# A graph attention kernel whose gather queue gets a memset and a drain after every gather

## The reference

```
edge layer 0 (4 heads of 32): kj = k[src] + e;  alpha = sum(q[dst] * kj) * scale
    softmax of alpha over the edges of each dst
    out[dst] = sum over edges of (v[src] + e) * alpha        then gate, project, layernorm -> x1
edge layer 1 (1 head of 256): scores = sum(q[dst] * k[src]) * scale + edge_weight * we + be
    softmax over the edges of each dst
    out[dst] = sum over edges of v[src] * attn               then layernorm, FFN, layernorm, layernorm
```

## Time and profile before

| | us |
|---|---|
| median of 3 executions | 5529.07 |
| lowest and highest | 5522.97, 5533.86 |
| span of the profiled execution | 6986.8 |
| of it before the first gather | 162.7 |
| first gather of phase 0 to its last | 3119.0 |
| from there to the first gather of phase 1 | 313.3 |
| first gather of phase 1 to its last | 2987.1 |
| from there to the end | 404.7 |
| busy: PE, DVE, POOL, ACT | 4413.6, 4304.2, 3716.2, 1729.7 |

### The profile page before, as it was taken

One profiled execution on the slowest core, in us unless ns is written; L12 is line 12 of the kernel. 1 busy time (PEld: TensorE's weight loads), 2 busy tenths in 40 slices (PEclk: granted clock), 3 DMA queues, 4 the chain that ended last, 5 costly groups with the idle time before them and its releaser, 6 DMA issues.

```text
span 6986.8 us, 104716 instructions
## 1 busy us (share of the span) xinstructions
PE 4413.6 (63%) x26899; PEld 3604.4 (52%) x26899; DVE 4304.2 (62%) x14756; ACT 1729.7 (25%) x4276; POOL 3716.2 (53%) x3934
## 2 busy tenths in 40 slices
PE   5565656565555556556656666666666666666698
PEld 3455555555555555555434555444454445555577
DVE  5456655566555556556855666666665666666688
ACT  0344544444444444445210000000000000000032
POOL 1555555555555555554135555556555555555455
PEclk9677776677777677777877778888887878878899
DMA  5565655555555555554345666556666666665422
GB/s 156 150 161 156 162 158 153 152 153 159 156 152 152 153 153 158 156 160 129 110 128 149 159 157 158 157 156 159 154 163 152 154 153 160 159 159 158 123 78 71
DMA packets 777208, 1039.58 MB, mean 149 GB/s; under 512 B 206912, under 2 KB 528273, under 8 KB 776609
## 3 DMA queue, kind: packets, MB, share of 16 engines
q1 hardware_dynamic: 466736, 499.53, 28.0%
q0 software_dynamic: 169040, 436.01, 23.3%
q10 hardware_dynamic: 140832, 97.33, 4.4%
HBM read 929.76 MB, written 128.40 MB: 151 GB/s over the span
## 4 chain that ended last, share of the span: by engine, by line
DVE 31%; PE 21%; another core or an unknown queue 19%; issue 15%; DVEq 6%; DMA 3%; POOL 3%; ACT 2%; ACTq 1%; POOLq 0%; SPq 0%
PE ps L1275 19%; DVE oh L1055 4%; DVE prod L925 4%; DVE rows L902 4%; POOL rows L580 3%; DVE acc L1075 2%; DVE score L914 2%; DMA acc_d<-acc 2%; DVEq L1133 2%; DVE msg L1050 2%; DVE oht L893 2%; DVE prod L909 1%; DMA rows<-x_d,idx 1%; DVEq L339 1%
## 5 line engine op out<-in xcount | busy, mean ns | idle before, releaser
L580 POOL DMA_INDIRECT rows<-kv_d,idx x1760 | 1709.4, 971 | 1552.0 <-DVE score L914 818.6
L580 POOL DMA_INDIRECT rows<-x_d,idx x1760 | 1767.7, 1004 | 1222.5 <-DVE score L925 581.2
L1275 PE MATMUL ps<-qw,oht 128*128 128x128 bf16 (+2 forms) x12320 | 1372.0, 267 | 230.4 <-issue 199.7
L1275 PEld LDWEIGHTS ps<-qw,oht 128*128 128x128 bf16 x12320 | 1125.8, 113 | 507.7 <-issue 294.2
L1275 PE MATMUL ps<-rows,oh 128*128 128x257 f32 x3520 | 1093.1, 469 | 421.8 <-DVE oh L1055 275.0
L1275 PEld LDWEIGHTS ps<-rows,oh 128*128 128x128 f32 x3520 | 789.9, 234 | 587.9 <-DVE oh L1055 302.3
L925 DVE CUSTOM_DVE_ANT_0 prod<-rows,ps 128x256 f32<-128x256 f32 x1760 | 637.1, 418 | 653.3 <-remote 229.6
L1275 PE MATMUL ps<-msg,oh 128*128 128x132 f32 x3520 | 679.0, 348 | 507.4 <-issue 296.1
L1275 PEld LDWEIGHTS ps<-msg,oh 128*128 128x128 f32 x3520 | 582.8, 246 | 575.2 <-issue 360.0
L699 ACT ACTIVATE pen_r<-ps 128x128 f32<-128x128 f32 (+1 forms) x110 | 29.9, 272 | 3051.3 <-PE ps L1355 2249.1
L1275 PE MATMUL ps<-w_c,ea 128*128 128x128 f32 x3520 | 691.0, 350 | 146.7 <-issue 103.3
(11 more groups left out here) (201 smaller groups left out, 4423.7 us busy)
## 6 DMA issues: line engine op xcount, KB each, us to landing
dst_row<-in_dst_row SPq DMA_DIRECT2D x880, 256.0 KB
qw<-q_d SPq DMA_DIRECT2D x440, 192.8 KB
acc_d<-acc ACTq DMA_DIRECT2D x440, 128.5 KB
ea<-in_eaT SPq DMA_DIRECT2D x440, 128.0 KB
qw<-q_d SPq DMA_DIRECT2D x440, 96.0 KB
acc_d<-acc ACTq DMA_DIRECT2D x440, 66.0 KB
rows<-kv_d,idx POOLq DMA_INDIRECT x1760
rows<-x_d,idx POOLq DMA_INDIRECT x1760
```

Of the source, the lines that this page charges most:

```text
L580: pool.indirect_dma_start(out=L.rows[par][:, st, j, 0:D], out_offset=None, in_=L.table, in_offset=bass.IndirectOffsetOnAxis(ap=idx[par][:, ...
L1275: return pe.matmul(out_, lhsT=lhsT, rhs=rhs, start=first, stop=last)
```

## The change

POOL gets a new buffer `spacer` of 128x384 f32 in SBUF, which nothing reads. After each gather, so 3520 times, it writes zeros to it and drains.

```diff
+SPACER = 384
...
+        spacer = sb("spacer", [P, SPACER])
...
                                 in_offset=bass.IndirectOffsetOnAxis(ap=idx[par][:, st, j:j + 1], axis=0),
                                 bounds_check=None if L is L0 else N - 1, oob_is_err=L is L0)\
                                 .then_inc(s["gathered"][b], 16)
+                            pool.memset(spacer[:, :], 0.0)
+                            pool.drain()
                 chunks(pool, emit)
```

## The result

The changed kernel takes 14469.66 us (14465.66 to 14484.62), the kernel before 5526.67 us beside it. The ratio is 2.619, 95% interval 2.616 to 2.623.

A forecast was written before the change was run, and what follows sets the result against it. The prediction took POOL as nearly full in both edge phases. Gathers of 4.7 and 4.8 us plus 0.3 us a pair gave 8404 and 8580 us, with 881 outside 17,865, rounded to 17,850; range 14,800 to 20,000.

The forecast's parts named there:

- the first rival: Drain in the loop waits only for POOL itself, not for the gather's packets: 8,500 us, chance 0.08.
- The preparation of 0.70 us: Ahead of each gather behind a drain, the next gather's preparation shows in full: 0.70 us in phase 0.
- some 1.3 us more: At each gather's drain: it ends 1.3 us after the gather's last packet, read from the drains ending both phases.
- The lower bound of 3.13 us: Gather start to drain end, calm case, from the last gather of phase 1; gave the total of 14,800 us.
- the drain ends with the landing: Rival for each gather's drain: it ends at the landing, 3.31 and 3.41 us a gather; 13,000 us, chance 0.05.
- 0.3 us a pair for the waits in the open: Ahead of each pair of four gathers, POOL's four waits and their arithmetic no longer hidden: 0.3 us, an estimate.
- Preparation in phase 1 of 0.80: Ahead of each phase 1 gather, preparation taken as 0.80 us because a bound for its indices is also set.
- Start to last packet 2.7 (2.5 + 0.2): Each gather's data is moved 2.5 us after its start, plus 0.2 us for meeting SP's loads.
- Outside the phases 881: Time ahead of, between and behind the two stretches of gathers, taken as unchanged: 881 us.
- The 0.2 us that I added for loads: Added to each gather's start to drain end, since some meet SP's loads on the same DMA engines: 0.2 us.
- The gathers that meet loads: Rival that every gather meets loads and takes 3.54 us to land, 5.6 and 5.7 in all: 20,900 us, chance 0.04.
- Not slower: Rival that the 0.30 us gap between gathers and POOL's room absorb memset and drain: 5,530 us, chance 0.01.

The follow-up runs named there:

- the second profile: The kernel before, unchanged, profiled once more: span 5549.3 us beside a time of 5550.99 us.

## Why the prediction was wrong

**What held.** POOL becomes the only bound, and the time is its distance between gathers times 3520 and the 861 us outside. The memset lies under the wait for the gather's data (the drain alone gives the same time, and so nearly do four memsets). The drain waits for the gather's transfer, not for POOL alone: the first rival's 8,500 us is far off. The preparation of 0.70 us is open behind each drain, to the hundredth. That POOL was nearly full before, which I argued from the plain time against the waits of the profile, is shown by the second profile and by the memsets of 256 and 384 columns.

**The step that failed.** "It waits until the gather's data has moved, and some 1.3 us more." The 1.34 and 1.33 us were measured right, but at drains with 1760 gathers ahead of them. I took them for a fixed part of every drain. The tail is 0.072 us behind the landing with one gather, grows by 0.04 us with each further one up to the 32 that were tried, and is 1.0 to 1.2 us at the end of a stage of the kernel before; between last packet and landing lie another 0.34 to 0.38 us. In the changed kernel the drain ends 0.44 us behind the last packet (mean), so 0.86 us too many stood in each of 3520 gathers: 3,030 us. The lower bound of 3.13 us from start to drain end came from such a drain too, with a tail of 1.21 us in it. Nor was it a calm gather, as I had it: it was one that moved no rows. From the gather's start to 6583.90 us POOL's DMA queue shows only 96 packets with 0.00 MB, all under 512 bytes:

```profile
q0 software_dynamic: 96, 0.00, 3.4%
```

By its semaphore the gather landed 1.95 us after its start. A short landing and a long tail happened to add up to 3.13. In the changed kernel the start to the drain's end takes 2.84 and 2.89 us in the median and 3.11 and 3.09 in the mean. That is why 14,800 was too high for a bound.

The first drain of line 239 was the hint. It has two transfers ahead of it, and ends 2.89 us after the start of the second (2.84 by the rounded rows), which took 2.76 us to land: a tail of 0.13 us, between those of one gather and of four. From it I made a rival, "the drain ends with the landing", at 13,000 us with a chance of 0.05. Its mechanism is the right one; its price took 2.61 us for the landing, from one of the two rows that I had (2.61 and 3.54), where the mean is 3.0.

**Smaller terms.** 0.3 us a pair for the waits in the open: 0.15 (130 us). Preparation in phase 1 of 0.80: 0.76 (70 us). Start to last packet 2.7 (2.5 + 0.2): 2.66 (140 us). Outside the phases 881: 861 (20 us). With the tail these take 17,865 to 14,475; measured were 14,470, and 14,483 in the profiled execution. The 0.2 us that I added for loads was about right: from median to mean the last packet is 0.24 and 0.19 us later.

**Other rivals.** The gathers that meet loads exist: 599 of 3520, one in six, take over 3.5 us to land (up to 6.5), and nearly all of these have packets of other queues beside them, 0.57 MB in the mean in phase 0, against 0.02 MB beside those that land within 3 us. They are not the rule that the rival made them. Not slower: that needed at most 0.07 us more for a gather, and the change brought 2.6.

On the page that spoke against the long drain, the Trainium skill, "Perfetto Trace Analysis", section "DMA Instruction — SWDGE (GPSIMD)": an instruction's record ends there when the last descriptor is written, not when the data has moved. The prediction put it as "before the data moves", which is more than the section says. In this trace it is so all the same: the record ends after 0.95 us, the first packet of the gather's queue starts 1.65 us after the gather (median, phase 0), the last ends at 2.4, and the landing comes at 2.8. The drain goes by the landing, which the section does not speak of.

## What to carry to other kernels

A drain on the queue that issues gathers is a wait for their landing: here every gather paid for its landing (2.8 us in the median, 3.0 in the mean) and for 0.7 us of preparation, which had both lain under other gathers before, and took 3.85 us in place of 1.25. Where a buffer has to be safe, wait for the one semaphore that says so, and only after further gathers are on their way, as the kernel before does with its wait for the pair before the last. Before a tail that one instruction shows is taken for a price, ask what had piled up ahead of that instruction; and when a profile's span is far from the plain time, take a second profile before its waits are read as room.

## What the runs showed that I had not expected

- A drain's end behind the landing grows by 0.041 us for each gather since the last drain (1, 4, 8 and 32 tried), though all but the last few have long landed. With 1760 it is 1.02 to 1.26 us where the drain already waits at the last landing, and 2.04 where it begins behind it. Where the growth stops, and what the drain does in this time, is open.
- A memset of one column (0.12 us) between two gathers is free, even with POOL full (1.25 us with and without). One of 256 columns costs 0.19 us; nothing between the two was tried.
- The same wait for a landing costs 0.5 us less ahead of a gather of phase 0 than of phase 1.
- One execution of the kernel before took 6986.8 us under the profiler at a granted TensorE clock of 0.779, another 5549.3 us at 0.865. PE was busy 4413.6 us in the first and 3924.2 in the second, DVE, ACT and POOL the same within 1%. What disturbed the first is open.
